# Scores of two head pairs issued back to back into four PSUM banks, in a 16-sequence transformer block on Trainium2

## The chip, the cores and the metric

The kernel runs on one core of one Trainium2 chip. A core has a matrix engine (TensorE, PE in the rows), a vector engine (VectorE, DVE), an activation engine (ScalarE, ACT), GpSimd (POOL) and a queue engine (SyncE, SP). Each runs its own instructions in the order in which they are written; semaphores make one wait for another. TensorE writes only to PSUM, which has eight banks of 512 fp32 columns by 128 partitions. The metric is the device time in microseconds (us) of one execution, and a kernel's time is the median of its runs.

## What is computed

Sixteen sequences of 256 rows by 128 columns go, each by itself, through two branches, whose sum is added to the input:

```
xn = layernorm(x)
y  = scan branch: depthwise conv -> dt = sigmoid(xf @ dt_w.T + dt_b) ...,
     16 states per channel: s = exp(dt*A)*s + dt*xt*b ; y = sum(s*c)
h  = layernorm(xn)*g + b ; q, k, v = h@Wq, h@Wk, h@Wv       (16 heads of 64)
q, k = l2norm(q)*q_scale, l2norm(k)*k_scale
attn = softmax(causal(10 * q @ k.T)) ; out = (attn @ v) @ Wo
h2 = layernorm(out)*g + b ; gate = softmax(h2 @ gate_w + gate_b)
moe = sum over 8 experts e: gate_e * (gelu(h2@w1_e + b1_e) @ w2_e + b2_e)
result = x + y + layernorm(moe)*g + b
```

## The kernel before

Everything stays on the chip; a sequence is two tiles of 128 rows. The program is a pipeline over sequences that is written out by hand. Body `i` (16 of them) has a **score phase** of ten steps `k` (0 to 9) and an **expert phase** of ten steps `m`. In the score phase of body `i` TensorE works on three things at once: attention of sequence `i` (eight pairs of heads, `p`), the projections of sequence `i+1`, and what is left of sequence `i-1` ahead of its experts (its scan states, its norm, its gate). In the expert phase it runs the eight experts of `i-1`, the output product of `i`, and the turned queries and keys of `i+1`. The first body has no older sequence, and the last one no newer one, so no projections.

The pieces of a score step on TensorE, with the short names used below:

- **S(p)**, `scores(i, p)` (lines 409 to 429): 16 matmuls for the two heads of a pair. A head has 64 columns, so each of these matmuls uses 64 of the array's 128 rows, and the two heads use the two halves. They write the two banks of `S2`, one per head, and `exps(i, p)` on ScalarE (line 716) takes the exponentials out of them into `P32`.
- **P(k)**, `project(i+1, k)` (lines 332 to 334): three fp16 matmuls over all 128 rows into bank `J[k % 2]`; ScalarE copies it (`copy_raw`, lines 666 and 668).
- **W(p)**, `weigh(i, p)` (line 444): twelve fp32 passes of exponentials by values into `O[p % 2]`. It waits for the causal cut of `P32` on GpSimd (`select`, line 877) and until `copy_ot(i, p-2)` has emptied that bank of `O`.
- **T(p)**, `turn_o(i, p)` (line 451): two transposes of the head outputs that VectorE has divided (`divide`, lines 1054 and 1057), into the same bank of `O`. `copy_ot(i, p)` on ScalarE (line 722) copies them out.
- **turn_max** (line 405) turns the row maxima, **turn_y** (line 469) the scan result of `i-1`, **turn_z2** (line 479) its normalised rows, and **gate_logits** (line 487) gives its gate logits.

Step `k` issues S(k), P(k), W(k-1), T(k-2), in this order; at `k = 0` there are also turn_max behind S(0) and turn_y behind P(0), and turn_z2 and gate_logits stand ahead of T in steps 3 and 5. Steps 8 and 9 hold two pieces of V projection each and no scores, so T(5) is followed by W(7) at once. Turned states, norm and logits are written to the banks `U[0]` and `U[1]`, which the experts use in the other phase. VectorE reads them with `add_y` (line 1191, in its step 4), `o_step` 6 (line 1077, step 4) and `o_step` 9 (line 1087, step 6). S(p) waits for `exps(p-1)`, since there is one pair of score banks.

GpSimd's order at the start of a body is `root_o(i-1)` (line 857; it needs `ove`, VectorE line 1071), `select(i, 0)`, `root_e`, `x_bias(i-1)` (line 884), `select(i, 1)`.

Of the kernel before, what the change touches and what calls it, by code (L numbers as in the profile page):

```python
# [40 lines left out]
def build(nc, x, a_log, b, c, dt_w, dt_b, conv_w, conv_b, ln_g, ln_b, Wq, Wk, Wv, q_scale, k_scale,  # L41
          Wo, gate_w, gate_b, w1, b1, w2, b2, out):
    ctx = ExitStack()
    with ctx:
# [115 lines left out]
        e2 = sb("e2", [P, T, D])  # L160
        xy = sb("xy", [P, T, D])
        fin = sb("fin", [P, T, D])
# [12 lines left out]
        J = [ctx.enter_context(nc.psum_tensor(f"J{n}", [P, 512], F32)) for n in range(2)]  # L175
        U = [ctx.enter_context(nc.psum_tensor(f"U{n}", [P, 512], F32)) for n in range(2)]

# [55 lines left out]
        def split_h2(s):  # L233
            return (hTh, hTl) if s == LAST else (h2h, h2l)

        def z2_bank(s):
            return J[0][:, 0:SEQ] if s == LAST else U[0][:, 0:SEQ]

        def logits_bank(s):
            return J[0][:, SEQ:SEQ + T * NE] if s == LAST else U[1][:, 0:T * NE]  # L240

# [3 lines left out]
        def y_bank(s):  # L245
            return S2[:, 1, 0:SEQ] if s == LAST else U[1][:, 0:SEQ]

# [68 lines left out]
        def _(pe):  # L316
# [92 lines left out]
            def scores(s, p):  # L409

                if p == 0:
                    pe.wait_ge(t_lo, (s + 1) * NL)
                    pe.wait_ge(mx_done, (s + 1) * 2 * NP)
                    pe.wait_ge(mt_done, 2 * s + 1)
                else:
                    pe.wait_ge(ex_done, s * NP + p)
                if p == NP // 2:
                    pe.wait_ge(mt_done, 2 * s + 2)
                g, hh = divmod(2 * p, 8)
                for kb in range(T):  # L420
                    for n in range(4):
                        for a in range(2):
                            r, q = slice(a * DH, (a + 1) * DH), slice(kb * P, SEQ)
                            keys = (sel[r, hh + a, :], KTh[r, p, kb * P:(kb + 1) * P],
                                    KTh[r, p, kb * P:(kb + 1) * P], KTl[r, p, kb * P:(kb + 1) * P])[n]
                            queries = (mT[r, g, q], QTh[r, p, q], QTl[r, p, q], QTh[r, p, q])[n]
                            last = mm(S2[:, a, kb * SEQ:kb * P + SEQ], keys, queries,  # L427
                                      start=(n == 0), stop=(n == 3), skip_group_check=True)
                last.then_inc(st_ready, 1)

            def weigh(s, p, before):

                pe.wait_ge(sel_done, s * NP + p + 1)
                if p == 0:
                    pe.wait_ge(v_done, (s + 1) * 2 * T)
                if p < 2 and before:
                    pe.wait_ge(acc_done, (s - 1) * NE * T - 2 * (1 - p))
                from_one(pe, ot_done, s * NP + p - 1)
                for t in range(T):
                    for a in range(2):  # L440
                        dst = O[p % 2][:, (2 * t + a) * VW:(2 * t + a + 1) * VW]
                        for kb in range(t + 1):
                            c0 = kb * SEQ + (t - kb) * P
                            last = mm(dst, P32[:, p % 3, a, c0:c0 + P], Vx[:, kb, 2 * p + a, :],  # L444
                                      start=(kb == 0), stop=(kb == t))
                last.then_inc(pv_done, 1)
# [17 lines left out]
            def turn_y(s):  # L464
                pe.wait_ge(y_done, (s + 1) * DS)
                if s < LAST:
                    from_one(pe, gelu_done, s * NE * FC)
                for t in range(T):
                    last = tr(y_bank(s)[:, t * P:(t + 1) * P], y[:, s % 2, t * P:(t + 1) * P], ident[:, :])
                last.then_inc(y_tr, 1)  # L470

            def turn_z2(s):
                pe.wait_ge(o_vec, s * KO + 7)
                if s < LAST:
                    from_one(pe, gelu_done, s * NE * FC)
                else:
                    pe.wait_ge(mt_done, 2 * s + 1)
                for t in range(T):
                    last = tr(z2_bank(s)[:, t * P:(t + 1) * P], z2[:, t, :], ident[:, :])
                last.then_inc(o_tr, 1)  # L480

            def gate_logits(s):
                pe.wait_ge(o_vec, s * KO + 8)
                if s < LAST:
                    pe.wait_ge(xy_done, s + 1)
                for t in range(T):
                    last = mm(logits_bank(s)[:, t * NE:(t + 1) * NE], h2T[:, t * P:(t + 1) * P], gws[:, :],
                              start=True, stop=True)
                last.then_inc(o_gate, 1)
# [19 lines left out]
            def expert_up(s, e):  # L509
                hi, lo = split_h2(s)  # L510
                for q in (2 * e, 2 * e + 1):
                    if q == 0:
                        pe.wait_ge(o_vec, s * KO + 10)
# [65 lines left out]
            def body(i, older, old, new, newer):  # L579
                for k in range(NP + 2):  # L580
                    if k < NP:
                        scores(i, k)
                    if k == 0:
                        turn_max(i, 1)
# [7 lines left out]
                    if old and k == 0:  # L592
                        turn_y(i - 1)
                    if old and k == 3:
                        turn_z2(i - 1)
                    if old and k == 5:
                        gate_logits(i - 1)
                    if k >= 2:
# [50 lines left out]
        def _(act):  # L649
# [63 lines left out]
            def exps(s, p):  # L713
                act.wait_ge(st_ready, s * NP + p + 1)
                from_one(act, pv_done, s * NP + p - 2)
                fn(P32[:, p % 3, :, 0:SEQ + P], S2[:, :, 0:SEQ + P], ACT.Exp).then_inc(ex_done, 1)  # L716

# [131 lines left out]
        def _(pool):  # L849
# [63 lines left out]
            def body(i, older, old, new, newer):  # L913
                for k in range(NP + 1):
# [4 lines left out]
                    if older and k == 0:  # L919
                        root_e(i - 2)  # L920
                    if old and k == 0:
                        x_bias(i - 1)
                    if newer and k == 4:
# [4 lines left out]
                if new:  # L928
                    for n in range(4):
                        units(i + 1, 1, n)  # L930

            def tail():
# [9 lines left out]
        def _(dve):  # L942
# [220 lines left out]
            def e_step(s, n):  # L1163
# [17 lines left out]
                else:  # L1181
                    dve.wait_ge(e_vec, at + 8)
                    dve.wait_ge(fin_free, 16 * (s + 1))
                    dve.wait_ge(xy_done, s + 1)
                    V.tensor_tensor(fin[:, :, :], e2[:, :, :], xy[:, :, :], ALU.add).then_inc(e_vec, 1)

            def add_y(s):
                dve.wait_ge(xb_done, s + 1)
                dve.wait_ge(y_tr, s + 1)
                from_one(dve, e_vec, s * KE)  # L1190
                V.tensor_tensor(xy[:, :, :].rearrange("p t d -> p (t d)"), y_bank(s),
                                xb[:, :, :].rearrange("p t d -> p (t d)"), ALU.add).then_inc(xy_done, 1)
# [79 lines left out]
            G_AT = {0: (0, 1), 3: (2,)}  # L1272
            O_AT = {1: (5,), 4: (6, 7), 5: (8,), 6: (9, 10, 11), 8: (12, 13)}
            O_LAST_AT = {2: (0, 1, 2), 3: (5,), 4: (6, 7, 8), 5: (9, 10, 11), 7: (12, 13), 8: (14,), 9: (15,)}
            SCAN_AT = {1: 0, 3: 1, 5: 2, 6: 3, 8: 4, 9: 5}

            def body(i, older, old, new, newer):
                for k in range(NP + 2):
# [15 lines left out]
                    if older:  # L1294
                        for n in E_AT.get(k, ()):
                            e_step(i - 2, n)
                    if old and k == 4:
                        add_y(i - 1)
# [96 lines left out]
```

## Time and profile before

| | |
|---|---|
| device time, median of 3 runs (lowest, highest) | 1157.72 us (1157.11, 1164.64) |
| span of the profiled execution, first to last instruction | 1155.9 us |
| TensorE matmuls busy | 1097.5 us, 95% |
| VectorE busy | 980.3 us, 85% |
| ScalarE busy | 786.9 us, 68% |
| GpSimd busy | 269.4 us, 23% |
| mean granted TensorE clock (1.0 is 2.4 GHz) | 0.979 |
| one middle body, start to start | 67.98 us |

A busy row of TensorE is longer than the time for which it holds the array: matmuls overlap, so what a piece costs is read from start to start of the pieces around it. The middle bodies repeat to a few hundredths of a microsecond, so that one of them (here the one whose score phase starts at 590.25 us) stands for all from 2 to 14.

### The profile page before, as it was taken

The page shows a single profiled execution, that of the slowest core. Times are in us where ns is not written, and L with a number is a line of the kernel's source. Part 1 is how long each engine was busy: PE and PEld are TensorE (multiplying, and loading weights), DVE is VectorE, ACT ScalarE, POOL GpSimd, SP SyncE. Part 2 cuts the span into 40 slices and gives each one's busy share as a digit, 9 for nine tenths or more (in the row PEclk, how much of TensorE's full clock was granted, in tenths as well). Part 3 has the DMA queues.
Part 4 walks back from the last instruction along what each step waited for, and adds up shares of the span by engine and source line. Part 5 has one row for each costly group of instructions (what it writes and reads, how often), then busy time and mean ns, then how long its engine had stood idle before and what let it go on. Part 6 is the DMA issues. An engine that isn't in the chain of part 4 may idle for free.

```text
span 1155.9 us, 27543 instructions
## 1 busy us (share of the span) xinstructions
PE 1097.5 (95%) x10435; PEld 915.9 (79%) x10435; DVE 980.3 (85%) x2576; ACT 786.9 (68%) x1772; POOL 269.4 (23%) x324
## 2 busy tenths in 40 slices
PE   4885999999999999999999999999999999999997
PEld 1573788888878888887888888788887888888897
DVE  7779789898898989889898988989899898988663
ACT  5582857768486775948667595866758587685553
POOL 2040312314041231404123130412303132130200
PEclk9795999999999999999999999999999999999899
DMA  7001000000000000000000000000000000000000
GB/s 204 6 1 41 6 6 11 1 11 6 6 11 2 15 2 11 6 6 11 1 16 2 6 10 7 11 1 15 2 6 10 6 11 1 11 2 1 11 2 10
DMA packets 18722, 14.60 MB, mean 13 GB/s; under 512 B 2408, under 2 KB 16160, under 8 KB 18592
## 3 DMA queue, kind: packets, MB, share of 16 engines
q1 hardware_dynamic: 17680, 12.76, 3.7%
q8 instruction: 84, 1.38, 0.5%
q14 instruction: 46, 0.38, 0.1%
q10 hardware_dynamic: 912, 0.09, 0.1%
HBM read 10.75 MB, written 2.10 MB: 11 GB/s over the span
## 4 chain that ended last, share of the span: by engine, by line
PE 86%; DVE 6%; issue 3%; POOL 2%; ACT 1%; POOLq 0%; DVEq 0%; ACTq 0%
PE O L539 19%; PE O L444 15%; PE S L427 7%; PE S L460 5%; PE U L523 5%; PE U L521 5%; PE U L522 5%; PE J L369 5%; PE J L332 4%; PE S L391 3%; PE J L333 3%; PE J L334 3%; PE S L387 3%; PE O L451 3%; DVE mxn L1048 1%
## 5 line engine op out<-in xcount | busy, mean ns | idle before, releaser
L743 ACT ACTIVATE hid<-U,b1c 128x256 f32<-128x256 f32 x512 | 200.6, 474 | 176.9 <-PE U L523 176.7
L539 PE MATMUL O<-w2s,hid 128*128 128x128 f32 x2048 | 251.0, 276 | 0.0
L539 PEld LDWEIGHTS O<-w2s,hid 128*128 128x128 f32 x2048 | 238.6, 192 | 2.9
L444 PEld LDWEIGHTS O<-Vx,P 128*128 128x128 f32 x1536 | 188.6, 192 | 35.3 <-issue 11.0
L444 PE MATMUL O<-Vx,P 128*128 128x66 f32 x1536 | 188.8, 273 | 11.5 <-ACT OT L722 9.0
L1150 DVE TENSOR_TENSOR_SCAN st<-aexp,u 128x256 f32<-128x256 f32 x256 | 175.5, 686 | 2.1 <-ACT aexp L728 2.0
L869 POOL TENSOR_TENSOR raw<-raw,nr 128x512 f32<-128x512 f32 x120 | 122.0, 1042 | 135.8 <-DVE nr L1013 135.8
L716 ACT ACTIVATE P<-S 128x768 f32<-128x768 f32 x128 | 103.7, 810 | 52.8 <-PE S L427 51.1
L877 POOL TENSOR_SCALAR_AFFINE_SELECT P<-P 128x512 f32<-128x512 f32 x128 | 90.9, 710 | 191.9 <-ACT P L716 191.9
L523 PE MATMUL U<-h2h,w1l 128*128 128x256 f16 x480 | 131.4, 274 | 0.0
L522 PE MATMUL U<-h2l,w1h 128*128 128x256 f16 x480 | 131.4, 274 | 0.0
L521 PE MATMUL U<-h2h,w1h 128*128 128x256 f16 x480 | 131.4, 274 | 0.0
L1160 DVE SCALAR_TENSOR_TENSOR y<-st,bc,y 128x256 f32<-128x256 f32 x240 | 122.1, 509 | 8.6
L857 POOL TENSOR_TENSOR orr<-ove,minus_half 128x2 f32<-128x2 f32 x16 | 11.2, 698 | 496.1 <-DVE ove L1071 496.1
L1048 DVE TENSOR_REDUCE mxn<-S 128x2 f32<-128x256 f32 x248 | 126.0, 551 | 0.1
L728 ACT ACTIVATE aexp<-dt,negA 128x256 f32<-128x256 f32 x256 | 116.6, 513 | 0.0
L1121 DVE SCALAR_TENSOR_TENSOR acc<-O,gate,acc 128x128 f32<-128x128 f32 x240 | 73.2, 347 | 47.3 <-PE O L539 44.7
L994 DVE TENSOR_REDUCE ssq<-sq 128x8 f32<-128x512 f32 x128 | 86.5, 676 | 1.9 <-ACT sq L668 1.9
L666 ACT ACTIVATE raw<-J 128x512 f32<-128x512 f32 x128 | 75.6, 591 | 5.2 <-PE J L334 5.1
L332 PE MATMUL J<-wh,hTh 128*128 128x512 f16 x188 | 74.0, 394 | 3.5 <-DVE hTl L990 2.8
L668 ACT ACTIVATE sq<-J 128x512 f32<-128x512 f32 x128 | 77.1, 602 | 0.0
L369 PE MATMUL J<-ident,raw 128*128 128x128 f32 x512 | 69.0, 278 | 6.5 <-DVE QTl L1033 3.4
(193 smaller groups left out, 2116.2 us busy)
## 6 DMA issues: line engine op xcount, KB each, us to landing
xin<-in_L_attn_x SPq DMA_DIRECT2D x16, 128.0 KB, 2.2
xres<-in_L_attn_x SPq DMA_DIRECT2D x16, 128.0 KB, 2.1
hid<-in_L_ffn_w SPq DMA_DIRECT2D x2, 1024.0 KB, 6.5
out_dram<-fin SPq DMA_DIRECT2D x16, 128.0 KB, 1.8
raw<-in_L_ffn_Wq SPq DMA_DIRECT2D x1, 512.0 KB, 4.4
raw<-in_L_ffn_Wk SPq DMA_DIRECT2D x1, 512.0 KB, 5.6
raw<-in_L_ffn_Wv SPq DMA_DIRECT2D x1, 512.0 KB, 6.5
wos<-in_L_ffn_Wo SPq DMA_DIRECT2D x1, 512.0 KB, 11.0
```

The source lines that it names most:

```text
L332: mm(dst, hi, wh[:, w0:w0 + 512], start=True, stop=False)
L369: last = tr(J[n % 2][:, (a * T + t) * P:(a * T + t + 1) * P], raw[:, chunk(t, kind, half), c0:c0 + P], ident[:, :])
L444: last = mm(dst, P32[:, p % 3, a, c0:c0 + P], Vx[:, kb, 2 * p + a, :], start=(kb == 0), stop=(kb == t))
L521: mm(dst, w1h[:, f:f + P], hi[:, :], start=True, stop=False)
L522: mm(dst, w1h[:, f:f + P], lo[:, :], start=False, stop=False)
L523: last = mm(dst, w1l[:, f:f + P], hi[:, :], start=False, stop=True)
L539: last = mm(O[e % 2][:, t * P:(t + 1) * P], hid[:, e % 2, m, t * P:(t + 1) * P], w2s[:, e * FC + m, :], start=(m == 0), stop=(m == FC - 1))
L743: fn(hid[:, e % 2, f % FC, :], U[q % 2][:, m * SEQ:(m + 1) * SEQ], ACT.Gelu_apprx_tanh, bias=b1c[:, f:f + 1], scale=1.0 / WS).then_inc(gel ...
L869: nc.gpsimd.tensor_tensor(group, group, nr[:, j * 8:(j + 1) * 8].unsqueeze(2).broadcast_to([P, 8, DH]), ALU.mult).then_inc(unit, 1)
L1048: V.tensor_reduce(mxn[:, t, g, hh:hh + DH + 2:DH + 1], max_bank(s, p)[:, :, t * P:(2 * t + 1) * P], AX.X, ALU.max, negate=True).then_inc(m ...
L1150: V.tensor_tensor_scan(st[:, d % 2, :], aexp[:, d, :], u[:, :], 0.0, ALU.mult, ALU.add).then_inc(scan_done, 1)
L1160: V.scalar_tensor_tensor(y[:, s % 2, :], st[:, d % 2, :], bc[:, d:d + 1], y[:, s % 2, :], ALU.mult, ALU.add).then_inc(y_done, 1)
```

## The change

Scores are issued in pairs in the even steps: S(k), S(k+1), and none in the odd steps. The even pair of heads uses the banks `S2` as before, the odd one the two banks of `U2` (the former `U[0]` and `U[1]`, declared as one). S(p) waits for `exps(p-2)` now. As `U` is taken, turned states go to `O[0]`, and the turned norm and the logits to `S2`: turn_z2 stands ahead of P(3) and waits for `exps(2)`; gate_logits stands ahead of P(5) and waits for `exps(4)`; S(4) waits until VectorE has read the norm, and S(6) until it has read the logits. W(0) waits for `add_y`. VectorE does `add_y` in step 0 and `o_step` 6 and 7 in step 3, 8 in step 4, 9 in step 5. `xy` has two buffers, and GpSimd does `x_bias(i)` at the end of body `i`.

```diff
-        xy = sb("xy", [P, T, D])
+        xy = sb("xy", [P, 2, T, D])
...
-        U = [ctx.enter_context(nc.psum_tensor(f"U{n}", [P, 512], F32)) for n in range(2)]
+        U2 = ctx.enter_context(nc.psum_tensor("U2", [P, 2, 512], F32))
+        U = [U2[:, n, :] for n in range(2)]
...
+        def score_bank(p):
+
+            return U2 if p % 2 == 1 else S2
...
-            return J[0][:, 0:SEQ] if s == LAST else U[0][:, 0:SEQ]
+            return J[0][:, 0:SEQ] if s == LAST else S2[:, 0, 0:SEQ]
...
-            return J[0][:, SEQ:SEQ + T * NE] if s == LAST else U[1][:, 0:T * NE]
+            return J[0][:, SEQ:SEQ + T * NE] if s == LAST else S2[:, 1, 0:T * NE]
...
-            return S2[:, 1, 0:SEQ] if s == LAST else U[1][:, 0:SEQ]
+            return S2[:, 1, 0:SEQ] if s == LAST else O[0][:, 0:SEQ]
...
-                else:
-                    pe.wait_ge(ex_done, s * NP + p)
+                elif p == 1:
+                    from_one(pe, gelu_done, (s - 1) * NE * FC)
+                    pe.wait_ge(v_done, 2 * T)
+                else:
+                    pe.wait_ge(ex_done, s * NP + p - 1)
+                if p == 4 and s > 0:
+                    pe.wait_ge(o_vec, (s - 1) * KO + 8)
+                if p == 6 and s > 0:
+                    pe.wait_ge(o_vec, (s - 1) * KO + 11)
...
+                if p == 0:
+                    from_one(pe, xy_done, s)
                 if p < 2 and before:
...
             def turn_y(s):
                 pe.wait_ge(y_done, (s + 1) * DS)
                 if s < LAST:
-                    from_one(pe, gelu_done, s * NE * FC)
+                    from_one(pe, acc_done, (s * NE - 1) * T)
...
                 for k in range(NP + 2):
-                    if k < NP:
+                    if k < NP and k % 2 == 0:
                         scores(i, k)
+                        scores(i, k + 1)
+                    if old and k == 3:
+                        turn_z2(i - 1)
+                    if old and k == 5:
+                        gate_logits(i - 1)
...
-                    if old and k == 3:
-                        turn_z2(i - 1)
-                    if old and k == 5:
-                        gate_logits(i - 1)
...
-                    if old and k == 0:
-                        x_bias(i - 1)
...
                     for n in range(4):
                         units(i + 1, 1, n)
+                    x_bias(i)
...
-            O_AT = {1: (5,), 4: (6, 7), 5: (8,), 6: (9, 10, 11), 8: (12, 13)}
+            O_AT = {1: (5,), 3: (6, 7), 4: (8,), 5: (9,), 6: (10, 11), 8: (12, 13)}
...
-                    if old and k == 4:
+                    if old and k == 0:
                         add_y(i - 1)
```

On TensorE, in steps 2 and 3 of a middle body, this stood before: T(0) (L451), S(3) (L427, eight rows), P(3).

```order
L451 MATMUL O<-ident,On 128x128 x2
L427 MATMUL S<-mT,sel 128x256 x2
L427 MATMUL S<-QTh,KTh 128x256 x2
L427 MATMUL S<-QTl,KTh 128x256 x2
L427 MATMUL S<-QTh,KTl 128x256 x2
L427 MATMUL S<-mT,sel 128x128 x2
L427 MATMUL S<-QTh,KTh 128x128 x2
L427 MATMUL S<-QTl,KTh 128x128 x2
L427 MATMUL S<-QTh,KTl 128x128 x2
L332 MATMUL J<-wh,hTh 128x512
L333 MATMUL J<-wh,hTl 128x512
L334 MATMUL J<-wl,hTh 128x512
```

After the change the same place reads as follows, from the last row of S(3) on. (Line numbers are those of the changed kernel: L439 is S, L337 to L339 P, L458 W, L465 T, L493 turn_z2.)

```order
L439 MATMUL U<-QTh,KTl 128x128 x2
L337 MATMUL J<-wh,hTh 128x512
L338 MATMUL J<-wh,hTl 128x512
L339 MATMUL J<-wl,hTh 128x512
L458 MATMUL O<-Vx,P 128x66 x6
L465 MATMUL O<-ident,On 128x128 x2
L493 MATMUL S<-ident,z 128x128 x2
L337 MATMUL J<-wh,hTh 128x512
L338 MATMUL J<-wh,hTl 128x512
L339 MATMUL J<-wl,hTh 128x512
L458 MATMUL O<-Vx,P 128x66 x6
L465 MATMUL O<-ident,On 128x128 x2
```

S(3) has moved ahead of P(2), W(1) and T(0), and between T(0) and W(2) only the turned norm and P(3) are left.

On VectorE, step 4 of a middle body began like this before: the division of W(2), the sums for the norm of queries and keys (`ssq`), then the turned states (`xy`) and the turned norm (`h2T`, `h2h`).

```order
L1054 RECIPROCAL rr<-O 128x4
L1057 TENSOR_TENSOR On<-O,rr 128x256
L994 TENSOR_REDUCE ssq<-sq 128x8
L1191 TENSOR_TENSOR xy<-U,xb 128x256
L1077 TENSOR_SCALAR h2T<-U,cols 128x256
L1081 CAST h2h<-h2T 128x256
```

After the change the turned norm is read one step earlier, behind the division of W(1) and the result of sequence `i-2` (`fin`), and ahead of `gve` and the scan of that step; `xy` has gone to step 0.

```order
L1070 RECIPROCAL rr<-O 128x4
L1073 TENSOR_TENSOR On<-O,rr 128x256
L1010 TENSOR_REDUCE ssq<-sq 128x8
L1201 TENSOR_TENSOR fin<-e,xy 128x256
L1093 TENSOR_SCALAR h2T<-S,cols 128x256
L1097 CAST h2h<-h2T 128x256
L988 TENSOR_SCALAR gve<-gmv 128x2
```

So what S(4) waits for is the fifth of these rows, and it stands one step ahead of where it stood.

## Rows read from the trace of the kernel before

**Rows 1.** The page, part 1: busy us, share of the span, instructions.

```profile
PE 1097.5 (95%) x10435; PEld 915.9 (79%) x10435; DVE 980.3 (85%) x2576; ACT 786.9 (68%) x1772; POOL 269.4 (23%) x324
```

**Rows 2.** Windows, middle body: busy PE, PEld, DVE, ACT, POOL; clock, DMA share, GB/s.

```profile
621.70:689.70 68.00, 67.33 (x654) 56.70 (x654) 60.20 (x160) 48.35 (x112) 17.25 (x20) 1.00 0.03 7
```

**Rows 3.** TensorE timeline, step 3: start us, duration us, line, tile; first and last scores.

```profile
598.46 0.28 PE L427 MATMUL S<-mT,sel 64*128 64x256 bf16 x2
...
599.08 0.22 PE L427 MATMUL S<-QTh,KTl 64*128 64x128 f16 x2
599.23 0.39 PE L332 MATMUL J<-wh,hTh 128*128 128x512 f16 x1
...
599.88 1.45 PE L444 MATMUL O<-Vx,P 128*128 128x66 f32 x12
601.17 0.39 PE L479 MATMUL U<-ident,z 128*128 128x128 f32 x2
601.39 0.38 PE L451 MATMUL O<-ident,On 128*128 128x128 f32 x2
601.71 0.28 PE L427 MATMUL S<-mT,sel 64*128 64x256 bf16 x2
```

**Rows 4.** TensorE timeline: T(6) into a projection; products for the maxima.

```profile
617.61 0.38 PE L451 MATMUL O<-ident,On 128*128 128x128 f32 x2
617.83 0.38 PE L332 MATMUL J<-wh,hTh 128*128 128x512 f16 x1
...
567.41 0.34 PE L387 MATMUL S<-KTh,QTh 64*128 64x128 f16 x4
567.68 0.40 PE L391 MATMUL S<-maskb,identb 128*128 128x128 bf16 x4
```

**Rows 5.** Timeline, steps 7 and 8: T(5), its copy on ScalarE, W(7).

```profile
613.95 0.39 PE L451 MATMUL O<-ident,On 128*128 128x128 f32 x2
614.90 1.52 PE L444 MATMUL O<-Vx,P 128*128 128x66 f32 x12 [0.57 <-ACT OT L722]
...
614.37 0.38 ACT L722 ACTIVATE OT<-O 128x256 f32<-128x256 f32 x1 [0.47 <-PE O L451]
```

**Rows 6.** Timeline, start of a body: S(0), GpSimd's and VectorE's work, W(0).

```profile
590.25 0.28 PE L427 MATMUL S<-mT,sel 64*128 64x256 bf16 x2
...
593.22 0.17 DVE L1172 TENSOR_SCALAR eve<-emv 128x2 f32<-128x2 f32 x1
593.26 0.63 POOL L877 TENSOR_SCALAR_AFFINE_SELECT P<-P 128x512 f32<-128x512 f32 x1
...
593.94 1.41 PEld L444 LDWEIGHTS O<-Vx,P 128*128 128x128 f32 x12 [0.60 <-POOL P L877]
```

**Rows 7.** VectorE timeline: division of W(1), result, later the states and the norm.

```profile
598.34 0.18 DVE L1054 RECIPROCAL rr<-O 128x4 f32<-128x4 f32 x1
...
599.49 0.41 DVE L1185 TENSOR_TENSOR fin<-e,xy 128x256 f32<-128x256 f32 x1
...
602.52 0.41 DVE L1191 TENSOR_TENSOR xy<-U,xb 128x256 f32<-128x256 f32 x1
602.85 0.54 DVE L1077 TENSOR_SCALAR h2T<-U,cols 128x256 f32<-128x256 f32 x1
```

**Rows 8.** ScalarE timeline of one score step.

```profile
599.34 0.81 ACT L716 ACTIVATE P<-S 128x768 f32<-128x768 f32 x1 [0.18 <-PE S L427]
...
601.00 0.92 ACT L728 ACTIVATE aexp<-dt,negA 128x256 f32<-128x256 f32 x2
601.81 0.38 ACT L722 ACTIVATE OT<-O 128x256 f32<-128x256 f32 x1
```

**Rows 9.** Last body: TensorE timeline, T(5) and W(7); a window behind them.

```profile
1086.07 0.39 PE L451 MATMUL O<-ident,On 128*128 128x128 f32 x2
1087.02 1.52 PE L444 MATMUL O<-Vx,P 128*128 128x66 f32 x12 [0.56 <-ACT OT L722]
...
1090.00:1092.00 2.00, 1.63 (x8) 1.26 (x9) 1.96 (x4) 0.89 (x2) 0.00 (x0) 0.50 0.00 0
```

More of the change, by code:

```diff
@@ L426, in scores @@
                             queries = (mT[r, g, q], QTh[r, p, q], QTl[r, p, q], QTh[r, p, q])[n]
-                            last = mm(S2[:, a, kb * SEQ:kb * P + SEQ], keys, queries,
+                            last = mm(score_bank(p)[:, a, kb * SEQ:kb * P + SEQ], keys, queries,
                                       start=(n == 0), stop=(n == 3), skip_group_check=True)
@@ L474, in turn_z2 @@
                 if s < LAST:
-                    from_one(pe, gelu_done, s * NE * FC)
+                    pe.wait_ge(ex_done, (s + 1) * NP + 3)
                 else:
@@ L484, in gate_logits @@
                 if s < LAST:
-                    pe.wait_ge(xy_done, s + 1)
+                    pe.wait_ge(ex_done, (s + 1) * NP + 5)
                 for t in range(T):
@@ L511, in expert_up @@
                 for q in (2 * e, 2 * e + 1):
+                    if q == 0 and s < LAST:
+                        pe.wait_ge(ex_done, (s + 2) * NP)
                     if q == 0:
@@ L715, in exps @@
                 from_one(act, pv_done, s * NP + p - 2)
-                fn(P32[:, p % 3, :, 0:SEQ + P], S2[:, :, 0:SEQ + P], ACT.Exp).then_inc(ex_done, 1)
+                fn(P32[:, p % 3, :, 0:SEQ + P], score_bank(p)[:, :, 0:SEQ + P], ACT.Exp).then_inc(ex_done, 1)
             def copy_ot(s, p):
@@ L1184, in e_step @@
                     dve.wait_ge(xy_done, s + 1)
-                    V.tensor_tensor(fin[:, :, :], e2[:, :, :], xy[:, :, :], ALU.add).then_inc(e_vec, 1)
+                    V.tensor_tensor(fin[:, :, :], e2[:, :, :], xy[:, s % 2, :, :], ALU.add).then_inc(e_vec, 1)
             def add_y(s):
@@ L1189, in add_y @@
                 dve.wait_ge(y_tr, s + 1)
-                from_one(dve, e_vec, s * KE)
-                V.tensor_tensor(xy[:, :, :].rearrange("p t d -> p (t d)"), y_bank(s),
+                from_one(dve, e_vec, (s - 1) * KE)
+                V.tensor_tensor(xy[:, s % 2, :, :].rearrange("p t d -> p (t d)"), y_bank(s),
                                 xb[:, :, :].rearrange("p t d -> p (t d)"), ALU.add).then_inc(xy_done, 1)
```

## The prediction, made before the changed kernel ran

> **What bounds the kernel now.** The page's first part comes first: TensorE's matmuls are busy for 95% of the span, VectorE for 85%, ScalarE for 68% [rows 1]. A share says little of a limit here, so the windows come next: in a middle body TensorE is busy for 67.33 of 68.00 us, at the full clock of 2.4 GHz (1.00), VectorE for 60.20 us [rows 2]. So a body is as long as TensorE's queue, and the change can give only what TensorE spends beside its matmuls. Where that is shows in the timeline, read from start to start.
>
> In step 3 [rows 3] the scores run from 598.46 to 599.08 and their last two matmuls hold the array 0.055 us more, 0.67 us in all; P starts at 599.23, 0.10 us late. P takes 0.65 us (599.23 to 599.88), W 1.29, a pair of transposes 0.22 (601.17 to 601.39), but the pair ahead of the next scores 0.32 (601.39 to 601.71), again 0.10 too much. Each S thus costs two gaps, 0.21 us. The products for the maxima say what makes the gap: four matmuls of 64 rows, by the same rates 0.17 us of work, take 0.27 until those of 128 rows begin (567.41 to 567.68), and T into a projection, fp32 into fp16 with all rows in both, costs 0.22 and no gap [rows 4]. The gap goes with the change between 64 and 128 rows.
>
> Two waits are left. Behind T(5), W(7) has nothing ahead of it: T starts at 613.95, its copy at 614.37, W at 614.90 [rows 5]. So from T to the W that needs its bank there are 0.95 us at least, with ScalarE at once at hand. And W(0) starts at 593.94, 3.69 us after S(0), when GpSimd's cut, begun at 593.26, is done [rows 6].
>
> **The change, part by part.**
>
> *Merged scores.* S(k), S(k+1) have no change of rows between them. Each pair saves one gap into and one out of the scores, 0.21 us. What follows T now is P, at no gap [rows 4]. There are four pairs in a body.
>
> *Pair 0 and 1.* W(0) still ends the wait: `root_o`, then the cut, hang on VectorE's work on the output rows, which the change leaves in its place. TensorE gets there earlier and waits longer; this pair's 0.21 us is lost. `add_y`, for which W(0) waits too, now stands behind `eve` (593.22 to 593.39) and takes 0.41 us as today [rows 6, 7]: done at about 593.8, ahead of the cut's end at 593.89, with about 0.1 us to spare. turn_y is issued by then (S, S, turn_max, P: about 2.4 us after S(0)), and `x_bias`, now at the end of the body before, long done. Body 0 has no `root_o` and keeps its 0.21.
>
> *Odd steps lose their cover.* T(k-3) is followed by P(k) and W(k-1), without scores. In step 7 TensorE reaches W(6) 0.22 + 0.65 = 0.87 us after T(4) began, and the copy allows 0.95: 0.08 us of wait, and a W that had to wait is 0.07 us longer (1.52 against 1.45) [rows 3, 5]. So 0.15 us goes back. In step 3 turn_z2 gives 0.22 more: 1.09, above 0.95, no wait; in step 5 the logits give at least as much. All this needs ScalarE at hand. One of its steps is 0.81 us from decay to copy and 1.66 from the exponentials to the decay [rows 8], with the copy about 2.8 of TensorE's 3.0 to 3.1; in an even step it is through with its decays 0.88 + 1.66 + 0.81 = 3.35 us after S(k) began (0.88 is the time from the start of S to its exponentials, 598.46 to 599.34), while T(k-2) begins at 0.77 + 0.67 + 0.65 + 1.29 = 3.38 us and its copy could begin 0.42 us later. ScalarE is there 0.45 us early.
>
> *The norm in the score bank.* S(4) waits for `h2T`. W(1) ends 3.38 us after S(2) began and VectorE starts its division 0.2 us later (598.34 today; W gives way to T at 598.46 - 0.32 = 598.14 [rows 3]). From there to the end of `fin` are 1.56 us (598.34 to 599.90), and `h2T` is 0.54 us [rows 7], so the read is over 3.58 + 2.10 = 5.7 us after S(2). S(4) comes at 3.38 + 0.22 + 0.22 + 0.65 + 1.29 + 0.32 = 6.1 us. 0.4 us to spare, so nothing. S(6) has more: VectorE reads the logits before the scan of step 5.
>
> *VectorE.* `add_y` moves from step 4 to step 0 and costs 0.41 us in either place; the buffer for `xy` takes the wait for `fin` from it. VectorE is then 0.34 us later in steps 0 to 2, ends `e*grow` before W(1) is through, and nothing waits there. In step 6 the division of W(5) comes only just ahead of T(5); up to 0.1 us could be lost.
>
> *The rest of a body.* From T(5) on the order is unchanged, and TensorE is nowhere waiting more than today; what the score phase saves reaches the span.
>
> *The last body* has no P at all. T to W is 0.95 there as well [rows 9], and now between T(0) and W(2) stand 0.44 us, T(2) and W(4) a little more, T(4) and W(6) 0.22: waits of 0.51, some 0.4 and 0.73, less three times 0.21: about 1.0 us lost.
>
> **The sum.** Bodies 1 to 14: 2 x 0.21 + (0.21 - 0.15) = 0.48 us each, 14 x 0.48 = 6.7. Body 0, with neither norm nor logits for cover: 0.21 + 3 x 0.06 = 0.4. Last body: -1.0. Together 6.1 us less. The profiled span is 1155.9 us, so 1149.8; the median of the runs lies 1.8 us above that span, and 1157.7 - 6.1 = 1151.6. About 1% (11.6 us) is what a measurement of this kernel can tell from no change.
>
> **Bounds of what no row shows.** S behind S in other banks: at best no gap, at worst the 0.10 us of rows 3, which is 4 x 0.10 x 16 = 6 us, all of the gain; I take none, since within one S the same change of operand shows none. The wait at W(6): nothing, or the 0.15 above plus ScalarE's lateness.
>
> **The rivals.**
>
> *No wait at W(6)* (the copy is a little quicker when P hides it): 0.63 us a body, 14 x 0.15 = 2.1 more saved, 1149.5. Against it: 0.95 stands alike in two bodies [rows 5, 9].
>
> *ScalarE comes late to the copies.* Its work in a pair of steps, 5.5 us and about 0.5 for the key norms, nears TensorE's 6.0 to 6.3. If the copies start 0.3 us late, W(2) loses 0.17 + 0.07 and W(6) 0.3: a body loses 0.06 instead of gaining 0.48, and with the last body the time is about 1159. For it: ScalarE has one fixed order in which T(k-2)'s copy stands ahead of the exponentials. Against: the 0.45 us above.
>
> *The gap belongs to the wait, not to the rows.* Then the second S pays it too, and only the new waits stay: 0.15 x 14, three such in body 0, and 1.6 in the last, 4 us in all, so 1162. Against: T into P and P into W wait as well and show no gap [rows 3, 4]. The Trainium skill, TensorEngine Tiling (Array Packing), Key Properties, says that a change of the tiling mode drains TensorE; by it this rival is out, and the sum above stays.
>
> *The other side: VectorE holds S(4).* TensorE would stand until the norm is read, once in each of 15 bodies. If VectorE is late by d, a body pays d - 0.4; it decides against the change from d = 0.4 + 0.48 = 0.9 us on. Were the read to come 1.4 us late, one scan and its addition, the price is 15 x 1.0 - 6.1 = 8.9 us, so 1166.6. For it: VectorE is the second busiest engine, and what stands ahead of it in step 3 runs without a gap. Against: the scan stands behind the read.
>
> *The clock falls earlier in the last body.* It is at half speed from 1090 [rows 9], behind the waits for W(7) and T(6). More waits ahead of them could bring that forward to W(7) at 1087.02, whose 1.4 us would double: 1153. The Trainium skill, TensorE: Matmul & The Clock Gate, part 1, says that the gate follows how busy TensorE was lately; in middle bodies a wait of 0.57 us leaves the clock at 1.00 [rows 2, 5].
>
> **Chances and numbers.** The forecast, 1151.6 with its own range of 1149 to 1154.5: 0.55. No wait at W(6): 0.12. ScalarE late: 0.09. Gap with the wait: 0.07. VectorE holds S(4): 0.09. Earlier fall of the clock: 0.08. A range of 1147 to 1160 leaves out VectorE's case, part of the gap's and what the measurement adds. Faster by over 1% (below 1146.1) needs 0.73 us in each body, more than four gaps less the wait (0.69): 0.08. Slower by over 1% (above 1169.3) needs 1.2 us of new waits a body: 0.08. Within 1%: 0.84.
>
> **What would show it.** Right: the second S of a pair starts 0.67 us behind the first; P follows T 0.22 us on; W(0) still 3.69 us after S(0), ended by the cut; W(6) 0.95 us after T(4); a middle body of 67.5 us. Wrong: scores of pair 4 or 6 that wait for VectorE, W(2) that waits for a copy, W(0) that waits for `xy`, or a middle body at or above 67.98 us.

## Result and profile after

The changed kernel takes 1169.03 us (median of 15 runs, 1166.65 to 1175.29), the kernel before beside it 1158.37 (15 runs, 1156.87 to 1164.79): a ratio of 1.0078, 95% interval 1.0057 to 1.0099. It is 0.8% slower, where 0.5% faster was predicted, and lies outside the range. The profiled execution spans 1164.9 us against 1155.9, so +9.0 us.

The runs of the kernel before lie near 1157 or near 1164.5 us, and its profile shown ahead of the prediction is of the first kind; those of the changed kernel reach from 1166.65 us, the one profiled here (granted clock 0.974), to 1175.29 (0.963).

The page's first part, busy time and share, answers [rows 1]; the window of a middle body (body 8, from S(0) to the next S(0); columns as in [rows 2]) answers [rows 2].

```profile
PE 1096.2 (94%) x10435; PEld 921.5 (79%) x10435; DVE 978.9 (84%) x2576; ACT 785.7 (67%) x1772; POOL 259.5 (22%) x324
```

```profile
594.57:662.57 68.00, 66.75 (x653) 56.78 (x653) 60.03 (x160) 48.25 (x110) 16.36 (x20) 1.00 0.03 8
```

In a body TensorE's matmuls take 66.75 us in the place of 67.33, so 0.58 us of work or gaps did go away. The body is still 68.00 us (67.98 before): the saving has become a wait. And some bodies are longer than that. From one S(0) to the next, bodies 1 to 14 take 69.23 us, thirteen times 67.55 to 67.99 before. After, body 1 takes 70.98, bodies 3 and 4 71.27 and 69.60, bodies 9 and 10 71.29 and 69.60, and the other nine 67.57 to 68.15.

**What came as predicted.** TensorE's timeline (start, duration, tile): the first and the last scores of the first S, the first and the last of the second, turn_max; then T(0) of step 2 with turn_z2 and P(3) of step 3, which answers [rows 3, 4].

```profile
594.57 0.28 PE L439 MATMUL S<-mT,sel 64*128 64x256 bf16 x2
...
595.18 0.22 PE L439 MATMUL S<-QTh,KTl 64*128 64x128 f16 x2
595.24 0.27 PE L439 MATMUL U<-mT,sel 64*128 64x256 bf16 x2
...
595.85 0.22 PE L439 MATMUL U<-QTh,KTl 64*128 64x128 f16 x2
596.00 0.44 PE L410 MATMUL J<-ident,mxn 128*128 128x128 f32 x2
```

```profile
603.14 0.39 PE L465 MATMUL O<-ident,On 128*128 128x128 f32 x2
603.36 0.38 PE L493 MATMUL S<-ident,z 128*128 128x128 f32 x2
603.58 0.38 PE L337 MATMUL J<-wh,hTh 128*128 128x512 f16 x1
```

The second S starts 0.67 us behind the first, with no gap, and the 0.10 us stands once, ahead of turn_max (596.00 where 595.90 would follow). T, turn_z2 and P follow each other at 0.22 us, no gap.

**Where it went wrong.** The timelines of TensorE, VectorE and GpSimd over steps 6 and 7 of the same body; the bracket is the idle time ahead and what ended it. The last line is VectorE's division of W(5) in the kernel before; it goes with T(5) there (613.95), the first of [rows 5].

```profile
615.41 0.39 PE L465 MATMUL O<-ident,On 128*128 128x128 f32 x2
616.37 1.52 PE L458 MATMUL O<-Vx,P 128*128 128x66 f32 x12
618.24 0.44 PE L465 MATMUL O<-ident,On 128*128 128x128 f32 x2 [0.35 <-DVE On L1073]
619.24 1.52 PE L458 MATMUL O<-Vx,P 128*128 128x66 f32 x12 [0.56 <-ACT OT L739]
```

```profile
610.85 1.11 DVE L1166 TENSOR_TENSOR_SCAN st<-aexp,u 128x256 f32<-128x256 f32 x1
...
612.40 0.17 DVE L1070 RECIPROCAL rr<-O 128x4 f32<-128x4 f32 x1
...
615.60 2.04 DVE L1112 TENSOR_SCALAR gl<-gl,gm 128x8 f32<-128x8 f32 x2
617.55 0.17 DVE L1070 RECIPROCAL rr<-O 128x4 f32<-128x4 f32 x1
617.76 0.42 DVE L1073 TENSOR_TENSOR On<-O,rr 128x256 f32<-128x256 f32 x1
```

```profile
615.57 2.05 POOL L886 TENSOR_TENSOR raw<-raw,nr 128x512 f32<-128x512 f32 x2 [0.91 <-DVE nr L1029]
```

```profile
613.14 0.43 DVE L1057 TENSOR_TENSOR On<-O,rr 128x256 f32<-128x256 f32 x1
```

W(6) starts 0.96 us after T(4), as predicted. W takes 1.36 us up to what follows it when that does not wait (607.73 to 609.09 in e1), so T(5) could start at 617.73; it starts at 618.24, 0.51 us late, because its division ends at 618.18 (the 0.35 in the bracket counts from the end of W's row, 617.89). VectorE is behind all the way there: from 612.40 to 618.18 it works without a break, and 2.04 us of that are two subtractions of 128x8 elements (L1112), which ran beside two of GpSimd's scalings (615.57 to 617.62); in the kernel before the pair took 1.82 us, so it was slow there too. There the same division ended at 613.57, 0.38 us ahead of T(5). TensorE now gets to T(5) 0.55 us earlier after S(0) (23.15 in place of 23.70 us, see e1), while the division ends 0.29 us later after S(0) (23.61 in place of 23.32; why is read below, in the part on the prediction).

Behind T(5) W(7) waits for its copy, as it did. TensorE thus stands twice within 1.5 us (617.73 to 619.24), and in five bodies its clock then falls. The windows of body 8, from 23.5 us after S(0), and of body 3 at the same place (clock: third column from the end):

```profile
618.07:619.57 1.50, 0.77 (x5) 0.56 (x6) 1.47 (x5) 0.86 (x3) 1.50 (x3) 1.00 0.00 0
619.57:621.57 2.00, 2.00 (x16) 1.39 (x16) 1.54 (x6) 1.79 (x8) 0.64 (x1) 1.00 0.03 8
```

```profile
273.23:274.73 1.50, 0.78 (x5) 0.58 (x5) 1.47 (x5) 0.87 (x3) 1.50 (x3) 0.94 0.00 0
274.73:276.73 2.00, 2.00 (x11) 2.00 (x11) 1.54 (x6) 1.65 (x7) 0.63 (x1) 0.50 0.00 0
276.73:278.73 2.00, 2.00 (x7) 0.84 (x7) 1.93 (x6) 0.39 (x1) 0.00 (x0) 0.50 0.00 0
...
280.73:282.73 2.00, 2.00 (x13) 1.25 (x12) 1.10 (x3) 1.24 (x3) 0.00 (x0) 0.84 0.00 0
```

The waits are alike (0.77 and 0.78 us busy of 1.50). Body 8 keeps the full clock of 2.4 GHz; body 3 works at half, 1.2 GHz, from W(7) on for some 7 us, and is 3.27 us longer; body 9 does the same, and in bodies 1, 4 and 10 the clock is low for some 3.4 us.

**The 9.0 us.** Bodies 3, 4, 9 and 10: 3.27 + 1.60 + 3.29 + 1.60 = 9.76 more than 68.00. Body 1, with the same fall: +1.75. The other nine of bodies 2 to 14, and those four at 68.00: 0.34 in all. Prologue and body 0: -0.93 and -1.45; both differ by such amounts between kernels in which nothing was changed there. Last body and tail: -0.42. Sum 9.05, as the spans give it unrounded (1164.92 and 1155.87).

### The profile page after: what moved, and what is told of

Read it like the earlier page. It is cut to its first block, busy times and chain, and to the rows that moved or that the text cites. A ratio compares the mean times of both kernels' runs of the same rounds, so it can differ in the third digit from the quotient of the medians.

```text
span 1164.9 us, 27589 instructions
## 1 busy us (share of the span) xinstructions
PE 1096.2 (94%) x10435; PEld 921.5 (79%) x10435; DVE 978.9 (84%) x2576; ACT 785.7 (67%) x1772; POOL 259.5 (22%) x324
## 4 chain that ended last, share of the span: by engine, by line
PE 75%; DVE 15%; issue 6%; POOL 2%; ACT 1%; POOLq 0%; DVEq 0%; ACTq 0%
PE O L555 19%; PE O L458 11%; PE S L474 5%; PE U L537 5%; PE U L538 5%; PE U L539 5%; PE J L374 4%; PE S L396 3%; PE J L337 3%; PE S L392 3%; DVE st L1166 3%; PE S L439 2%; PE J L338 2%; PE J L339 2%; PE O L465 2%
## 5 line engine op out<-in xcount | busy, mean ns | idle before, releaser
L458 PEld LDWEIGHTS O<-Vx,P 128*128 128x128 f32 x1536 | 190.4, 195 | 45.2 <-issue 22.8
L458 PE MATMUL O<-Vx,P 128*128 128x66 f32 x1536 | 193.8, 277 | 16.5 <-ACT OT L739 10.2
L1166 DVE TENSOR_TENSOR_SCAN st<-aexp,u 128x256 f32<-128x256 f32 x256 | 180.5, 705 | 1.8 <-ACT aexp L745 1.7
L894 POOL TENSOR_SCALAR_AFFINE_SELECT P<-P 128x512 f32<-128x512 f32 x128 | 83.9, 656 | 208.6 <-ACT P L733 208.6
L337 PE MATMUL J<-wh,hTh 128*128 128x512 f16 x188 | 76.5, 407 | 3.3 <-DVE hTl L1006 2.8
L338 PE MATMUL J<-wh,hTl 128*128 128x512 f16 x188 | 75.3, 400 | 0.0
```

Of the source, the lines that this page charges most:

```text
L1166: V.tensor_tensor_scan(st[:, d % 2, :], aexp[:, d, :], u[:, :], 0.0, ALU.mult, ALU.add).then_inc(scan_done, 1)
```

## Experiments

The short names of the experiments are those of the texts on record. Times compare with those of the kernel before on the same chip. For e1 to e4 these have a median of 1163.9 us (21 of them, 1155.14 to 1164.91), so bodies and spans are compared rather than ratios. Bodies are read from one profiled execution of each kernel.

**e1: take the cause of the late division away.** VectorE's gate maximum and its subtraction move from step 6 to step 7, behind the division of W(5).

```
-  O_AT = {1: (5,), 3: (6, 7), 4: (8,), 5: (9,), 6: (10, 11), 8: (12, 13)}
+  O_AT = {1: (5,), 3: (6, 7), 4: (8,), 5: (9,), 7: (10, 11), 8: (12, 13)}
```

> One edit to the changed kernel: VectorE does o_step 10 and 11 (maximum of the gate logits and its subtraction, whose two small instructions take 2.04 us there) in step 7, behind the division of W(5), and no longer in step 6 ahead of it. Theory A (VectorE's queue holds the division of W(5), so T(5) starts 0.51 us late in each middle body, and this wait together with the one at W(7) lets TensorE's clock fall in some bodies): T(5) starts at once behind W(6), 23.15 us after S(0) and not 23.66; a middle body takes 67.5 us and not 68.00; the clock stays at 1.00 from body 2 to 14; about 1149 us (1146 to 1153). Theory B (the clock falls because of the merged scores, whatever T(5) does): middle bodies of 67.5 us, but two or four bodies again 1.6 to 3.3 us longer at half clock, about 1159 us. Theory C (T(5) waits for something else): no change, about 1168 us.

Measured 1150.93 us (1147.64 to 1156.33), ratio 0.9918 [0.9890, 0.9947], span 1145.9. TensorE's timeline from T(5), and the window of body 8:

```profile
609.09 0.39 PE L465 MATMUL O<-ident,On 128*128 128x128 f32 x2
610.04 1.52 PE L458 MATMUL O<-Vx,P 128*128 128x66 f32 x12 [0.56 <-ACT OT L739]
```

```profile
585.94:653.37 67.43, 66.53 (x653) 56.70 (x653) 59.40 (x160) 48.26 (x110) 16.36 (x20) 1.00 0.03 8
```

T(5) waits for nothing and starts 23.15 us after S(0); the wait for W(7) is as before; a middle body is 67.44 us, and no body from 2 to 14 has a fall. So the late division costs both: the 0.56 us of each body, and the falls. That holds for the profiled execution (1147.64 us, granted clock 0.981); the others of e1 had 0.972 to 0.981, and no profile shows where.

**e7: the same edit in the kernel before**, a control: is e1's gain the lateness alone?

```
-  O_AT = {1: (5,), 4: (6, 7), 5: (8,), 6: (9, 10, 11), 8: (12, 13)}
+  O_AT = {1: (5,), 4: (6, 7), 5: (8,), 6: (9,), 7: (10, 11), 8: (12, 13)}
```

> The kernel before with the gate maximum and its subtraction on VectorE in step 7 in the place of step 6, the edit that took 0.56 us from each middle body of the changed kernel. Theory (the gain there is only the lateness that the change brought in, since in the kernel before the division of pair 5 ends 0.38 us ahead of T(5)): no change, middle body 67.95 to 68.00, 1157 to 1158 on the scale of 1157.7. Rival (the edit is a gain of its own): middle body 67.4 to 67.7, 1149 to 1153, and then the merged scores are worth less than 0.5 us a body.

Measured 1157.48 us (1156.85 to 1165.01), ratio 0.9994 [0.9963, 1.0026]; a middle body 67.98, T(5) at 23.70. No change: there the division was early enough. The merge alone is therefore worth 67.98 - 67.44 = 0.54 us a body. The profiled execution spans 1162.9 us, 7.0 more than that of the kernel before. Its middle bodies are the same; 5.1 of the 7.0 us lie in its last body (95.31 us in place of 90.17), the rest in bodies 0 and 1. In the last body the clock is at 0.50 for 13.7 us from W(0) on; a window of that stretch:

```profile
1073.60:1079.60 6.00, 6.00 (x48) 4.77 (x47) 3.07 (x9) 1.99 (x4) 0.64 (x1) 0.50 0.08 22
```

**e6: is it GpSimd that makes the subtraction slow?** GpSimd's four scalings of the first half go from steps 6 and 7 to steps 7 and 8; VectorE keeps its order.

```
-  if new and k in (6, 7):
-      units(i + 1, 0, 2 * k - 12)
-      units(i + 1, 0, 2 * k - 11)
+  if new and k in (7, 8):
+      units(i + 1, 0, 2 * k - 14)
+      units(i + 1, 0, 2 * k - 13)
```

> The changed kernel with GpSimd's four scalings of the first half of the raw queries and keys (units) one step later, so that they no longer run beside VectorE's subtraction of the gate maximum. Theory (that subtraction takes 2.04 us in the place of 0.36 because GpSimd works beside it, and so makes the division of pair 5 late): subtraction near 0.4 us, T(5) 0.5 us earlier, no fall of the clock, middle body 67.4 to 67.5, 1149 to 1152. Rival (VectorE is late through the scan and addition ahead, whatever GpSimd does): T(5) stays at 23.6 us after the body's start, middle body 68.0, falls as in the changed kernel, about 1166 to 1169.

Measured 1155.82 us (1153.46 to 1157.38), ratio 0.9965 [0.9945, 0.9985]. VectorE's and GpSimd's timelines and T(7):

```profile
612.38 0.36 DVE L1112 TENSOR_SCALAR gl<-gl,gm 128x8 f32<-128x8 f32 x2
...
616.72 1.73 DVE L1120 TENSOR_SCALAR gate<-ge,grs 128x8 f32<-128x8 f32 x2
```

```profile
614.37 4.05 POOL L886 TENSOR_TENSOR raw<-raw,nr 128x512 f32<-128x512 f32 x4
```

```profile
620.17 0.44 PE L465 MATMUL O<-ident,On 128*128 128x128 f32 x2 [0.32 <-DVE On L1073]
```

The subtraction takes 0.36 us, T(5) is on time (23.15 us after S(0)), no fall: as expected to there. But the body is 67.97, not 67.4 to 67.5: the scalings now lie beside the next pair of small operations, the gates (L1120), which take 1.73 us in place of 0.36, and T(7) waits for the division behind them, 2.00 us after T(6) in place of 1.51. The cost moved by four microseconds. What makes such an operation slow is GpSimd beside it: each of the two gates, as each of the two subtractions in the changed kernel, ends some 0.03 us behind the GpSimd scaling then under way. The Trainium skill, SBUF — State Buffer, "SBUF: two separate sides", calls the pair of ports that VectorE and GpSimd share an exclusive lock, held for a whole instruction; the trace agrees in that two operations of 128x8 take as long as the two scalings beside them (2.04 and 2.05 us).

**e5: the late T(5) without the merge.** The kernel before, with one addition of 128x768 elements on VectorE ahead of the division of W(5); its result is not used.

```
+  if old and k == 7:
+      dve.wait_ge(d_w2, 16)
+      V.tensor_tensor(late[:, :], w2s[:, 0:6, :]..., w2s[:, 6:12, :]..., ALU.add)
   if k >= 2:
       divide(i, k - 2)
```

> The kernel before with one more VectorE addition of 128x768 (its result is used nowhere) ahead of the division of pair 5 in bodies 1 to 15, so that T(5) there comes late as in the changed kernel, with scores, projection and banks as before. The division now ends 0.38 us ahead of T(5); the addition should take 0.8 to 0.9 us, so T(5) starts about 0.5 us late and W(7) waits 0.57 more behind it. Theory (two waits one behind the other are what lets TensorE's clock fall, whatever the order of the scores): a middle body of 68.5 us, 7 us in all, and on top some bodies that are 1.6 to 3.5 us longer with the clock at 0.50 behind W(7): about 1167 to 1180. Rival (the merged scores or the new order cause the falls): all middle bodies at 68.5, clock 1.00 behind W(7), about 1164.7 on the scale of 1157.7.

Measured 1171.05 us (1170.45 to 1171.66), ratio 1.0082 [1.0050, 1.0115], span 1169.8. TensorE's timeline in body 9 from T(5), and its windows there:

```profile
691.20 0.44 PE L452 MATMUL O<-ident,On 128*128 128x128 f32 x2 [0.38 <-DVE On L1058]
692.20 1.52 PE L445 MATMUL O<-Vx,P 128*128 128x66 f32 x12 [0.56 <-ACT OT L723]
```

```profile
692.00:694.00 2.00, 1.80 (x14) 1.64 (x15) 1.58 (x6) 2.00 (x9) 1.10 (x2) 0.93 0.03 8
694.00:696.00 2.00, 2.00 (x7) 0.72 (x5) 1.93 (x5) 0.80 (x2) 0.00 (x0) 0.50 0.00 0
```

Middle bodies are 68.57, as the late T(5) makes them; bodies 1, 4 and 9 take 71.52, 70.76 and 70.21, with the clock at 0.50 behind W(7). The scores, banks and order are those of the kernel before. So the two waits one behind the other are enough for the falls (here of some 3.4 us each), and the merge is not needed for them. In how many bodies the clock falls, and in which, is not explained: 5 of 14 in the changed kernel, 3 of 14 here. In body 4 T(5) came 0.56 us later still; elsewhere the waits of bodies with and without a fall read alike.

**e2, e3: take the other wait away.** W(7) gets work ahead of it: the first projection of the values (project_v(0)) goes ahead of W(7), the third behind T(6), and on ScalarE the last copy of raw and the gate's exponentials go ahead of the decays, so that the bank is free. e2 does that in the changed kernel, with the late T(5) left in; e3 in the kernel before.

```
 PE  + if new and k == NP: project_v(i + 1, 0)      (ahead of weigh)
     + if new and k > NP:  project_v(i + 1, 2)
     - if new and k >= NP: project_v(i + 1, 2 * (k - NP))   (behind weigh)
 ACT + at k == NP - 1, behind copy_ot(i, NP - 3): copy_raw(i + 1, NP - 1); gate_exps(i - 1)
     - copy_raw(i + 1, k - 1) at k == NP, gate_exps(i - 1) at k == 7 behind the decays
```

> The changed kernel with cover for the wait of W(7) and nothing done about T(5): TensorE issues the first V projection of step 8 ahead of W(7), and ScalarE does copy_raw(7) and the gate's exponentials right behind the copy of T(5), ahead of the last two decays, so that the V projection finds its bank free. Theory A: T(5) is still 0.5 us late, but the 0.65 us of V projection now stand in the wait behind it: a middle body of 67.35 to 67.45 us, and with only one wait of 0.5 us left at this place the clock does not fall; about 1147 to 1151 us. Theory B: middle bodies of 67.4 us but some again at half clock, 1156 us or more. If the wait of W(7) only moves on to the second V projection, the body stays at 68.0 us.

> The same cover for W(7) in the kernel before (no merged scores, no other bank). A middle body of 67.98 - 0.6 = 67.35 to 67.4 us, so 14 or 15 bodies give 9 us: about 1149 us. If the wait of W(7) is only moved on, 1158 us.

e2: 1151.86 us (1150.96 to 1153.99), ratio 0.9912 [0.9883, 0.9942], middle body 67.62. e3: 1150.40 us (1148.66 to 1165.74), ratio 0.9914 [0.9879, 0.9949], middle body 67.60. TensorE's timeline in e2 from T(5):

```profile
612.26 0.44 PE L465 MATMUL O<-ident,On 128*128 128x128 f32 x2 [0.35 <-DVE On L1078]
...
613.27 1.52 PE L458 MATMUL O<-Vx,P 128*128 128x66 f32 x12
...
615.27 0.38 PE L465 MATMUL O<-ident,On 128*128 128x128 f32 x2
615.81 0.39 PE L337 MATMUL J<-wh,hTh 128*128 128x512 f16 x1 [0.15 <-ACT Vx L700]
```

T(5) is as late as in the changed kernel, but W(7) no longer waits, and no body from 2 to 14 has a fall. With e1, where T(5) is on time and W(7) waits, either wait alone leaves the clock at 1.00 in the bodies 2 to 14 that were profiled. The gain of the cover is 0.38 us and not the 0.6 that both expectations gave: 0.32 us comes back behind T(6), where the next projection (615.81, where 615.49 would follow) waits for ScalarE's copy out of its bank.

**e4: e1 and the cover together.**

> The changed kernel with both edits: o_step 10 and 11 behind the division of W(5), and cover for W(7). Theory A: a middle body of 66.85 to 66.95 us (0.5 us below the cover alone in either kernel), no fall of the clock from body 2 to 14, about 1140 us (1137 to 1144). This would beat both kernels. Theory B: as long as the kernel before with cover, or longer, 1149 us or more.

Measured 1146.43 us (1143.08 to 1147.92), ratio 0.9866 [0.9820, 0.9912]; window of body 8:

```profile
583.70:650.76 67.06, 66.57 (x653) 56.74 (x652) 59.80 (x160) 48.04 (x110) 16.36 (x20) 1.00 0.03 8
```

67.06 us, so the merge (with its division on time) is worth 67.60 - 67.06 = 0.54 us a body here too; the cover fell short by about as much as in e2. The time misses the 1137 to 1144 us expected: by the body (66.85 to 66.95 expected), and in the profile by a last body of 90.50 us (88.20 in e1), in which the clock falls twice to 0.50.

**e8, e9: the wait of W(0).** Was the 0.21 us of pair 0 and 1 lost, as the prediction had it, on the wait for GpSimd's cut? In e8 (on e4) the cut goes ahead of root_o, and add_y behind the first expert statistic; in e9 (on e3, without the merge) the cut alone goes ahead. The part of the edit that both share:

```
-  if old and k == 0: root_o(i - 1)
   if k < NP: select(i, k)
+  if old and k == 0: root_o(i - 1)
```

> The changed kernel with the later gate maximum and the covered W(7), and in step 0 GpSimd's cut of pair 0 ahead of root_o, with VectorE's add_y behind the first expert statistic in the place of behind eve. What ended W(0)'s wait (3.71 us after S(0)) was the cut, queued behind root_o; the exponentials are there 1.68 us after S(0), so the cut can end at 2.35, add_y at about 3.2, and TensorE arrives behind its projections at 3.22. Theory (the 0.21 us of pair 0 and 1 was lost only on GpSimd's queue): W(0) at 3.2 to 3.35, middle body 66.6 to 66.7 in the place of 67.06, about 6 us in all, 1139 to 1142. Rival (the gain goes into a later wait of the score phase, at W(2) or at S(4) for h2T): W(0) earlier, but a middle body of 66.9 to 67.06, 1144 to 1147.

> The kernel before with the covered W(7) and the cut of pair 0 ahead of root_o, without merged scores. TensorE waits 0.60 us there for the cut, and nothing but the cut stands behind root_o. Theory (the wait is GpSimd's order alone, and the merge's gain in pair 0 and 1 is independent of it): W(0) at 3.1 us after S(0), middle body 67.0 to 67.05 in the place of 67.60, 1142 to 1144, and the changed kernel with the same edits still shorter by 0.35 to 0.45 us a body. Rival (VectorE or ScalarE hold W(0) as well): W(0) at 3.4 to 3.69, middle body 67.3 to 67.6, 1147 to 1151.

e8: 1138.36 us (1137.46 to 1138.96), ratio 0.9813 [0.9775, 0.9851], middle body 66.78. e9: 1145.48 us (1144.49 to 1145.80), ratio 0.9873 [0.9827, 0.9919], middle body 67.23. W(0) and what stands ahead of it in the changed kernel (S(0) at 594.57, with add_y), in e8 (S(0) at 583.00, with the cut and add_y), then e8's window of that body, and in e9 (S(0) at 587.24):

```profile
597.57 0.38 PE L339 MATMUL J<-wl,hTh 128*128 128x512 f16 x1
597.65 0.42 DVE L1207 TENSOR_TENSOR xy<-O,xb 128x256 f32<-128x256 f32 x1
598.29 1.55 PE L458 MATMUL O<-Vx,P 128*128 128x66 f32 x12 [0.34 <-POOL P L894]
```

```profile
586.00 0.38 PE L339 MATMUL J<-wl,hTh 128*128 128x512 f16 x1
586.46 1.52 PE L458 MATMUL O<-Vx,P 128*128 128x66 f32 x12
...
584.76 0.63 POOL L899 TENSOR_SCALAR_AFFINE_SELECT P<-P 128x512 f32<-128x512 f32 x1 [30.35 <-ACT P L736]
...
585.82 0.42 DVE L1212 TENSOR_TENSOR xy<-O,xb 128x256 f32<-128x256 f32 x1
```

```profile
583.00:649.79 66.79, 66.55 (x654) 56.74 (x654) 59.66 (x160) 48.00 (x110) 16.42 (x20) 1.00 0.03 8
```

```profile
590.45 0.38 PE L334 MATMUL J<-wl,hTh 128*128 128x512 f16 x1
590.66 1.45 PE L444 MATMUL O<-Vx,P 128*128 128x66 f32 x12
```

In the changed kernel TensorE's projections end at 597.79 and W(0) starts 0.50 us later. In e8 the cut ends at 585.39 and holds nothing any more; W(0) starts 0.24 us after the projections, 0.22 after add_y's end (586.24), so VectorE now ends that wait (in e8's last body add_y ends 0.12 us earlier after S(0), and so does W(0)'s wait). The same holds, within 0.01 us, for the changed kernel: W(0) starts there 0.06 us behind the cut's end (598.23) but also 0.22 behind add_y's (598.07), so cut and add_y were level, and by these rows moving the cut alone would have gained next to nothing (not run). The body gains 0.28 us of the 0.36 to 0.46 expected, none of it given back later; the time is below the 1139 to 1142 expected all the same, as the last body is 87.01 us, without the two falls that e4's has. In e9 W(0) follows the projections at once, 3.42 us after S(0). The expectation of 3.1 was wrong: the 0.60 us it used stand on the row of the weight load in [rows 6]; by the row of the projection the wait in the kernel before was 0.26 us. With its own form of these edits the merged kernel remains 67.23 - 66.78 = 0.45 us a body ahead.

## Why the prediction failed

**Right: the gaps.** 0.21 us a pair, T into P at 0.22 us, the second S at 0.67 us. A body was to gain 0.48; with the division on time it gains 0.54 (e1 against e7, e4 against e3), and e1's 1150.93 us is near where the prediction put the changed kernel (1151.6). That the time agrees is in part luck: in e1's profile the last body is 1.97 us shorter than before (88.20 in place of 90.17), where 1.0 was to be lost, because the later fall of the clock [rows 9] is absent.

**Right: W(6), the banks, ScalarE, and W(0) in its time.** W(6) starts 0.96 us after T(4); neither S(4) nor S(6) waits for VectorE. The copies start with their transposes in time. W(0) starts 3.70 to 3.72 us after S(0) in the middle bodies (3.89 in body 12). The profile puts its wait down to the cut, but add_y, which was to have 0.1 us to spare, was level with it (e8), so the sign "W(0) that waits for `xy`" is not ruled out.

**Wrong: "In step 6 the division of W(5) comes only just ahead of T(5); up to 0.1 us could be lost."** It is 0.51 us, all of the gain. The prediction shows no working for the 0.1 and leaves it out of the sum. It equals the 0.48 us by which T(5) was to come earlier less the 0.38 us that the division had to spare; read so, it supposes that the division stays where it was after S(0), and it does not. VectorE's divisions of W(3), before and after, and the two subtractions before:

```profile
604.62 0.18 DVE L1054 RECIPROCAL rr<-O 128x4 f32<-128x4 f32 x1 [0.90 <-PE O L444]
609.40 0.18 DVE L1070 RECIPROCAL rr<-O 128x4 f32<-128x4 f32 x1 [0.91 <-PE O L458]
611.20 1.82 DVE L1096 TENSOR_SCALAR gl<-gl,gm 128x8 f32<-128x8 f32 x2
```

In both kernels VectorE waits for W(3) and then works without a break to the end of the division of W(5): 8.95 us before, 8.78 after. W(3) now has two pairs of scores ahead of it, S(4) and S(5), in place of one, so this run starts 14.83 us after S(0) in place of 14.37. T(5) comes 0.55 us earlier and the run that leads up to it starts 0.46 later; against these 1.01 us stand the 0.38 to spare and 0.17 of shorter work. That leaves 0.46, and 0.05 more pass from the end of the division to T(5). On the way W(4) is through at 611.72 (T(3), behind it, starts there), but the scan and addition of step 5 keep VectorE until 612.40. The rival on VectorE looked at S(4), where it had room, and not at the division, where it had none.

**Wrong: "From T(5) on the order is unchanged, and TensorE is nowhere waiting more than today".** The waits did not grow from T(5) on, but one more came right ahead of an old one, and the clock answered. The prediction let the clock fall only in the last body; that a wait of 0.57 us alone leaves it at 1.00 was right (and held in e1) but said nothing of two. This made "no gain" into +9 us; e5 shows it without the merge, e1 and e2 show it gone when either wait goes.

**The last body.** Up to T(5) it was to lose 1.0 us; in e1 T(5) there comes 21.20 us after S(0), against 20.37, so 0.83. In the profile of the changed kernel it comes at 22.76, since the clock falls behind the wait for W(0), which is 1.63 us there. This fall is not the merge's alone: in e1 the clock stays at 1.00 behind the same wait, and in e7, with the scores of the kernel before, it falls behind one of 1.13 us. The row of W(0), the window from W(0) on, and that of the stretch that was at 0.50 in the kernel before [rows 9]:

```profile
1078.88 1.72 PE L458 MATMUL O<-Vx,P 128*128 128x66 f32 x12 [1.63 <-POOL P L894]
```

```profile
1078.80:1083.00 4.20, 4.12 (x44) 3.48 (x44) 3.06 (x9) 1.91 (x5) 1.50 (x4) 0.66 0.02 4
```

```profile
1099.50:1105.50 6.00, 4.40 (x41) 4.03 (x40) 5.34 (x13) 3.57 (x12) 0.00 (x0) 1.00 0.01 3
```

The later fall is gone, and the last body and tail are 0.42 us shorter in all.

**The range** had no case in which the middle bodies gain nothing and some lose over 3 us. The rival with VectorE, left outside it at 1166.6 us, lies near the measured time by luck: it had VectorE hold S(4), which never waits, and no fall of the clock. The sign that did come true is a middle body at or above 67.98 us (68.00).

## What to carry over

Before a queue is shortened by so much a stage, read for each of its waits how early the other engine's result is there now: it becomes a wait as soon as the gain is larger than that spare time, here 0.38 us against 0.55. Read also when the other engine can begin: the same reordering let VectorE start 0.46 us later. Put the smallest operations of VectorE where GpSimd is idle, and where they can't be, behind what TensorE waits for. And judge a new wait by its neighbours: two waits of 0.5 us one behind the other cost more than their sum, so it pays to place one of them apart, or to give one of them cover, even when the stage as a whole gets no shorter.

## What the runs showed of the hardware

- Two waits of TensorE of 0.5 and 0.56 us within 1.5 us let its clock fall to 1.2 GHz, in 5 of 14 bodies of one kernel (for some 3.4 us in three, some 7 us in two) and in 3 of 14 of another (some 3.4 us each), at 1.6 to 3.3 us a fall. With one of them alone, or with the second some 4.5 us behind the first (e6), it did not fall in bodies 2 to 14 of five kernels (before, e1, e2, e6, e7). Each is one profiled execution.
- Two VectorE operations of 128x8 elements take 0.36 us with GpSimd idle. Begun beside GpSimd's products of 128x512 they take as long as what GpSimd has under way: the subtractions 1.82 us in the kernel before, 2.04 in the changed one, 1.27 in e1, the gates 1.73 in e6. A scan takes 0.68 us alone and 1.11 where the cut began 0.06 us ahead of it (step 5 of the changed kernel); where the scan began first (606.31 in the kernel before, the cut at 606.49) it kept its 0.68 and the cut took 0.93 in place of 0.64.
- Behind the same wait of 1.13 us for W(0) in the last body the clock stayed at 1.00 in the profile of the kernel before and fell to 0.50 for 13.7 us in that of e7, whose order on TensorE is the same; that body was 5.1 us longer. What decides between the two is not shown.
